# Out-projection, second normalisation, routing and sending of sequences 0 to 2 inside the attention of a transformer-like kernel on one core

## What is computed

```python
def attention(x):                      # x: (4, 1024, 128), H = 16, HD = 8
    q, k, v = (x @ W + b for each), split in heads
    scores = q.k / sqrt(8) + slope * -|kpos - qpos|, causal
    return softmax(scores).v @ Wo + bo
def moe(inputs):                       # rows n of all four sequences in one order, C = 512
    probs = softmax(x @ Wr + br); gate = max(probs); idx = argmax(probs)
    pos = cumsum(one_hot(idx)) * one_hot(idx); keep = pos < C
    h = relu((gate * x in slot pos of expert idx) @ W1 + b1); eo = h @ W2 + b2
    return gate * eo[idx, pos]
x = x + attention(layernorm(x));  x = x + moe(layernorm(x))
x = x + L1_attn(layernorm(x));    x = x + L1_ffn(layernorm(x))
```

## Time and profile before

| | |
|---|---|
| median of three runs | 726.85 us |
| profiled execution | 730.23 us, of which the span of instructions is 728.5 us |
| mean granted TensorE clock over the span | 0.867 |
| TensorE, VectorE, ScalarE, GpSimd busy over the span | 528.9, 494.2, 440.7, 243.0 us |
| last weighted sums copied | 494.9 us |
| chain that ended last, by engine | PE 43%, DVE 21%, POOL 13%, ACT 9% |

### The profile page before, as it was taken

One profiled execution on the slowest core, in us unless ns is written; L12 is line 12 of the kernel. 1 busy time (PEld: TensorE's weight loads), 2 busy tenths in 40 slices (PEclk: granted clock), 3 DMA queues, 4 the chain that ended last, 5 costly groups with the idle time before them and its releaser, 6 DMA issues.

```text
span 728.5 us, 13724 instructions
## 1 busy us (share of the span) xinstructions
PE 528.9 (73%) x4883; PEld 245.3 (34%) x4883; DVE 494.2 (68%) x964; ACT 440.7 (60%) x800; POOL 243.0 (33%) x403
## 2 busy tenths in 40 slices
PE   3675888889988998998889889884776019006774
PEld 2441333333333233332323332212665017004654
DVE  4999788889888888898888889400776206116553
ACT  1970478778877887787778778760245005007872
POOL 2651121122122122112214511210215744758552
PEclk9995699999999999999999999965775559656996
DMA  7488546522323340453232030001112133112012
GB/s 170 109 167 261 112 109 160 123 60 49 83 46 76 78 109 16 101 126 75 60 79 53 10 79 11 10 4 37 58 44 74 53 122 142 32 50 78 16 45 58
DMA packets 64906, 57.30 MB, mean 79 GB/s; under 512 B 12209, under 2 KB 55590, under 8 KB 64828
## 3 DMA queue, kind: packets, MB, share of 16 engines
q1 hardware_dynamic: 56152, 50.15, 27.8%
q10 hardware_dynamic: 6128, 2.90, 1.5%
q0 software_dynamic: 2560, 3.39, 1.4%
HBM read 29.40 MB, written 29.69 MB: 81 GB/s over the span
## 4 chain that ended last, share of the span: by engine, by line
PE 43%; DVE 21%; POOL 13%; ACT 9%; issue 9%; DMA 4%; SPq 1%; DVEq 0%; POOLq 0%; ACTq 0%
PE sums L772 16%; DVE neg_max L799 11%; PE ring L751 11%; ACT probs L820 6%; PE bank L723 6%; POOL x_rows L1044 3%; POOL expert_rows L1038 2%; PE bank L717 2%; DVE probs L517 2%; POOL rs L1059 1%; ACT xn L1485 1%; DVE v_all L525 1%; PE ring L734 1%; DMA denominators<-weighted_sums 1%; POOL max_parts L870 1%
## 5 line engine op out<-in xcount | busy, mean ns | idle before, releaser
L799 DVE TENSOR_REDUCE neg_max<-bank 128x2 f32<-128x1024 f32 (+2 forms) x320 | 342.9, 1115 | 62.0 <-PE bank L723 59.9
L820 ACT ACTIVATE probs<-ring 128x512 f32<-128x512 f32 (+4 forms) x481 | 301.9, 681 | 81.1 <-PE ring L751 68.6
L751 PE MATMUL ring<-q_operand,k_operand 56*128 56x512 bf16 (+3 forms) x768 | 165.3, 335 | 18.7 <-ACT probs L820 14.7
L772 PE MATMUL sums<-probs,v_all 128*9 128x512 f32 (+3 forms) x1536 | 164.8, 502 | 2.1 <-POOL probs L853 1.5
L853 POOL TENSOR_SCALAR_AFFINE_SELECT probs<-probs 128x512 f32<-128x512 f32 x128 | 80.2, 635 | 218.4 <-ACT probs L820 217.9
L723 PE MATMUL bank<-k_operand,q_operand 54*128 54x512 bf16 (+3 forms) x768 | 144.9, 339 | 6.9 <-DVE v_all L525 5.3
L751 PEld LDWEIGHTS ring<-q_operand,k_operand 56*128 56x128 bf16 x768 | 50.2, 94 | 154.9 <-ACT probs L820 112.6
L717 PE MATMUL bank<-masks 64*128 64x128 bf16 (+2 forms) x768 | 71.7, 223 | 5.3 <-DVE neg_max L799 4.9
L723 PEld LDWEIGHTS bank<-k_operand,q_operand 54*128 54x128 bf16 x768 | 45.9, 97 | 24.6 <-DVE neg_max L799 15.2
L717 PEld LDWEIGHTS bank<-masks 64*128 64x128 bf16 x768 | 36.5, 95 | 38.2 <-DVE neg_max L799 25.8
L772 PEld LDWEIGHTS sums<-probs,v_all 128*9 128x9 f32 x1536 | 23.3, 89 | 53.6 <-issue 40.4
(11 more groups left out here) (152 smaller groups left out, 681.5 us busy)
## 6 DMA issues: line engine op xcount, KB each, us to landing
q_operand<-q_rows SPq DMA_DIRECT2D x64, 96.0 KB, 3.7
k_operand<-k_rows SPq DMA_DIRECT2D x32, 192.0 KB, 4.4
q_rows<-qk_parts SPq DMA_DIRECT2D x36, 128.0 KB, 2.4
k_rows<-qk_parts SPq DMA_DIRECT2D x36, 128.0 KB, 2.4
expert_rows<-fill SPq DMA_DIRECT2D x16, 258.0 KB, 5.7
rows<-expert_rows SPq DMA_DIRECT2D x8, 516.0 KB, 6.5
weighted_sums<-osum SPq DMA_DIRECT2D x128, 18.0 KB
sums_in<-in_L_attn_x SPq DMA_DIRECT2D x4, 512.0 KB, 7.5
```

What stands on the lines that cost most here:

```text
L751: last = nc.tensor.matmul(psS[:, bank, w * j:w * j + w], k_op[rows, buf, p, P * kb:P * kb + P], q_op[rows, buf, c, p, q0:q0 + w], start=Tr ...
L772: last = nc.tensor.matmul(psO[32 * i:32 * i + HD + 1, q0:q0 + w], v_all[:, n, kb, i, :], probs[:, u % NPROBS, i // 2, i % 2, 0:w], start=u ...
L799: nc.vector.tensor_reduce(neg_max[:, n % 2, slot, kc, :, pairs[0]:pairs[-1] + 1, t % CH], src, AX.X, ALU.max, negate=True).then_inc(a_read, 1)
L820: nc.scalar.activation(dst, src, ACT.Exp).then_inc(ring_read, 1)
```

## The change

A fifth kind, `E`, enters the order: the entries of `EARLY_AT`, for each of sequences 0 to 2, at fixed units of the attention of the following groups. A position is (group - first group) x 12 + unit, the first group being 5, 9 or 13. The entry stands after that unit's `V`.

- The spreading of the reciprocals by matmul becomes two DMAs on SyncE: 64 KB to HBM (position 5) and 512 KB back, each head's row to eight partitions (position 7).
- `divide`, the addition of the projection, powers, scales, normalised rows and rows times gate go to GpSimd, which reads no PSUM, so ScalarE copies the projection into SBUF (`st`) first. GpSimd also issues the 8 sends of a sequence, at positions 28 to 35.
- Projection, transposes, logits and counts on TensorE take one turn each of the ring of three banks (2, 2, 1 and 1 per sequence); ScalarE copies every one of them out.
- Moments, choosing and placing stay on VectorE, in between its maxima. The counts of earlier sequences are kept as running sums, so one matmul replaces one per earlier tile.
- The clears of the slots follow the stores, one per `A`; residual rows are loaded at groups 4 to 7. The bias is added per sequence at positions 5 and 6, the last sequence's with that of sequence 2. The rows after the addition go to HBM in one DMA of 512 KB per sequence (position 21).
- The later block does sequence 3 alone, in the steps of before, without the loop of ticks. The buffers of the routing lie in a region that first holds the q and k parts of sequences 0 to 2.

```diff
+EARLY = B - 1
+EARLY_AT = {
+    4: [("reciprocals", 0)], 5: [("store_reciprocals", 0), ("bias", 0)], 6: [("bias", 1)], 7: [("load_reciprocals", 0)],
+    10: [("divide", 0)], 11: [("divide", 1), ("project", 0)], 12: [("project", 1)], 14: [("moments", 0)],
+    15: [("moments", 1), ("power", 0)], 16: [("power", 1)], 17: [("scales", 0)], 18: [("normal", 0)],
+    19: [("normal", 1), ("turned", 0)], 20: [("turned", 1)], 21: [("store_x1", 0)], 22: [("logits", 0)], 23: [("choose", 0), ("exps", 0)],
+    25: [("counts", 0)], 26: [("place", 0)], 27: [("gated", 0)], 28: [("gated", 1)],
+    **{28 + i: [("gated", 1)] * (i == 0) + [("send", i)] for i in range(KB)}}
...
+            b = (n - H // GH - 1) // (H // GH)
+            for name, c in EARLY_AT.get((n - H // GH - 1) % (H // GH) * NU + u, []) if 0 <= b < EARLY else []:
+                if name in TURNED:
+                    turn += 1
+                    order.append(("E", n, name, b, c, (head, held[head], turn)))
...
+                def load_reciprocals(b):
...
+                    sp.wait_ge(rden_out, 16 * (b + 1))
+                    sp.dma_start(r["rdb"], rden_dram[b].unsqueeze(0).to_broadcast([HD, H, S])).then_inc(rdb_in, 16)
...
-                    elif kind == "A" and n >= 5 and args[0] % 8 == 4 and clears:
+                    elif kind == "A" and clears:
                         clear_slots(sp, clears.popleft())
...
+                def project_early(b, c, bank):
...
+                    pe.wait_ge(at_ready, QC * b + c + 1)
+                    for i in range(CH):
+                        last = nc.tensor.matmul(psS[:, bank, P * i:P * i + P], ot[:, b, CW * c + P * i:CW * c + P * i + P],
+                                                w["wo"][:, :], start=True, stop=True)
+                    last.then_inc(ring_fill, 1)
...
+                def divide(b, c):
+                    pool.wait_ge(o_in[b], 32)
+                    pool.wait_ge(rdb_in, 16 * (b + 1))
+                    to = slice(CW * c, CW * c + CW)
+                    nc.gpsimd.tensor_tensor(ot[:, b, to], ot[:, b, to], r["rdb"][:, to], ALU.mult).then_inc(at_ready, 1)
+
+                def add_projected(b, c, turn):
+                    pool.wait_ge(ring_read, turn)
+                    pool.wait_ge(xb_ready, QC * b + c + 1)
...
+                def normal_early(b, c):
+                    k = QC * b + c
+                    for u in range(CH * k, CH * k + CH):
+                        last = nc.gpsimd.tensor_scalar(r["xn2"][:, u, :], rows[:, u, X1:X1 + D], r["mv2"][:, u, 0:1],
+                                                       r["nt2"][:, 1, u:u + 1], ALU.subtract, ALU.mult)
+                    last.then_inc(xn2_ready, 1)
...
+                def send(u):
...
+                    pool.wait_ge(row_ready, u + 1)
+                    nc.gpsimd.indirect_dma_start(
+                        out=slots_dram, out_offset=bass.IndirectOffsetOnAxis(ap=r["slot"][:, u:u + 1], axis=0), in_=rows[:, u, :],
+                        in_offset=None, bounds_check=E * CAP - 1, oob_is_err=False).then_inc(scattered, 16)
...
-        for u in range(TILES):
+        for u in range(KB * b, TILES):
             send_rows(u)
```

More of the change, by code:

```diff
@@ L130 @@
 VGROUP = 1
+EARLY = B - 1
[6 more added lines that the diff above has]
+    **{28 + i: [("gated", 1)] * (i == 0) + [("send", i)] for i in range(KB)}}
+TURNED = {"project": (1000, 600), "turned": (700, 600), "logits": (2000, 230), "counts": (900, 230)}
+EARLY_TIME = {"reciprocals": ("dve", 960), "moments": ("dve", 1450), "choose": ("dve", 2300), "place": ("dve", 2000),
+              "exps": ("act", 260), "bias": ("pool", 1200), "divide": ("pool", 1200), "power": ("pool", 1050),
+              "scales": ("pool", 1000), "normal": ("pool", 1600), "gated": ("pool", 1600), "send": ("pool", 1280)}
 def exp_items(u):
@@ L791, in _, with maxima @@
                 nc.vector.memset(psO, 0.0).then_inc(o_clear, 1)
-                for n in range(NG):
-                    if n >= 2:
+                def maxima(n, k):
+                    slot, t, kc, w, pairs = MAXUNITS[k]
+                    if n >= 2 and k == 0:
                         dve.wait_ge(cut_ready, QC * (n - 1))
[L796 to L804, removed]
@@ L892, in _ @@
                         cut_maxima(n, *args)
+                    elif kind == "E":
+                        name, b, c, use = args
+                        if name == "bias":
+                            add_bias(b, c)
+                            if b == EARLY - 1 and c == QC - 1:
+                                for last in range(QC):
+                                    add_bias(EARLY, last)
+                        elif name == "divide":
+                            divide(b, c)
+                        elif name == "project":
+                            add_projected(b, c, use[2])
+                        elif name == "power":
+                            power_early(b, c)
+                        elif name == "scales":
+                            scales_early(b)
+                        elif name == "normal":
+                            normal_early(b, c)
+                        elif name == "gated":
+                            gated_early(b, c)
+                        elif name == "send":
+                            send(KB * b + c)
         later_stages(nc, ctx, sb, sem, w, dict(
@@ L1005, in _ @@
     def _(sp):
-        for k in range(CHUNKS):
+        for k in LATE:
             sp.wait_ge(x1_ready, k + 1)
@@ L1192, in _ @@
-        dve.wait_ge(slot_ready, len(ROUNDS))
-        dve.wait_ge(row_ready, ROUNDS[-1][0])
-        for u in range(*ROUNDS[-1]):
+        divide(K0)
+        divide(K0 + 1)
+        for k in LATE:
+            add(k)
+        for k in LATE:
+            scales(k)
+        dve.wait_ge(fold_psum, 1)
+        nc.vector.tensor_copy(aqk[:, :], psFold[:, 0:P])
+        nc.vector.tensor_tensor(wft[:, :], psFold[:, P:2 * P], dis[:, :], ALU.add).then_inc(fold_ready, 1)
+        for k in LATE:
+            take_logits(k)
```

499 lines of the change are left out of this document (315 added, 184 removed).

## The result

| | time, us | profiled execution: span, us | granted clock, mean |
|---|---|---|---|
| before | 726.45 median (725.26 to 731.77) | 728.5 | see the earlier trace rows by stage |
| changed | 744.24 median (735.63 to 744.32) | 742.4 | 0.864 |

Changed over before: 1.0193, with a 95% interval from 1.0146 to 1.0239. The change makes the kernel about 14 us slower by this ratio (17.8 us between the medians), where 22 us less had been forecast (705).

A forecast was written before the change was run, and what follows sets the result against it. It took TensorE's fixed order, nearly full, to bound the attention and GpSimd's sends the end. 730.23 - 54 (end) + 32 (attention) = 708.2, by the median 705; own range 697 to 714, overall 690 to 724.

The forecast's parts named there:

- The end: Late part behind the attention: with only sequence 3 left there, the last send lands at 540.2 not 594.60, giving back 54 us.
- the walk: Step-by-step chain of sequence 3 from last reciprocal to last send's landing: about 34 us instead of 88, 3 us either way.
- The clears: Burst of 16 slot clears in the attention delays a DMA hop of the maxima once or twice: 1 us, between 0 and 6.
- The wait for the reciprocals' load: First half of a sequence: load lands in 5.3 us, so TensorE stands 1.5 to 2 us before the projection.
- GpSimd's 25 us a sequence: GpSimd's moved elementwise work and sends in the attention, costed at nothing because idle time ahead of masks covers them.
- the rival that was given 0.11: GpSimd's queue in the attention: masks held behind waiting entries, V matmuls behind masks; 750 us at 0.5 each; chance 0.11.
- waits in TensorE's order: Attention: 18 new TensorE entries each wait about 1 us for another engine, 723 us, parity at 1.2 each; chance 0.17.
- TensorE, VectorE and ring turns: Moved work in the attention, per sequence: TensorE 2.3 us in the first half, both engines 5.5 in the second, banks 0.5.
- absorbed: Attention: the planner's order puts new work where engines idle, cost 12 us, time 685; chance 0.16.
- Clock 1.00 in the attention: TensorE's granted clock stays 1.00 through the attention, and its new work, 6.2 us a sequence, is priced at it.
- The port rival: Attention: VectorE's two-input instructions wait for GpSimd's elementwise work, 4 us a sequence, 12 in all, time 717; chance 0.10.

The follow-up runs named there:

- y0_after: The changed kernel as it is, run once more on another chip beside the kernel before: 747.21 us, ratio 1.0103 to the kernel before.
- x3_late_sends: Changed kernel with the 24 sends of sequences 0 to 2 moved from the attention to the last block: 756.51 us, ratio 1.0395 to the kernel before.
- x1_load: Changed kernel with the reciprocals' buffer filled once from a constant table, three loads and waits gone, denominators wrong: 724.66 us, ratio 0.9948 to the kernel before.
- y5_dma: Same kernel as x5_dma, run again beside y0_after: 736.51 us, ratio 0.9946 to the kernel before.
- x2_light: Changed kernel with normalised rows moved from GpSimd to ScalarE and gated rows to VectorE: 738.46 us, ratio 1.0159 to the kernel before.
- y6_all: Same kernel as x6_all, run again beside y0_after and y5_dma: 721.33 us, ratio 0.9763 to the kernel before.
- the first set: x1_load, x2_light, x3_late_sends and x4_both: edits of the changed kernel, one cause at a time or two together, 719.84 to 756.51 us.
- the third set: y0_after, y5_dma, y6_all and x9_warm: changed kernel, two reruns of variants and a clock test, 747.21, 736.51, 721.33 and 746.59 us.
- x7_double_pe: x6_all with each early projection, transpose and logits matmul issued twice: 737.18 us, 15.6 us over x6_all.
- x8_more_dve: x6_all with 48 more unused statistics instructions on VectorE in each of three sequences' moments: 727.35 us (two runs), 5.8 us over x6_all.
- x6_all: x5_dma plus x2_light's move of normalised rows to ScalarE and gated rows to VectorE: 721.6 us, ratio 0.9734 to the kernel before.
- x9_warm: Changed kernel with five unused matmuls ahead of TensorE's wait for each sequence's first divide: 746.59 us, ratio 1.0071 to the kernel before.
- x5_dma: Changed kernel with transfers reordered, reciprocals loaded one entry earlier and used later, no computation dropped: 736.8 us, ratio 0.9956 to the kernel before.
- x4_both: Changed kernel with the edits of x1_load and x2_light together, denominators wrong: 722.02 and 719.84 us, two far longer executions left out.

## Why the prediction was wrong, step by step

**The end (54 us): right.** 33.9 us against the walk's 34.0. The last eight sends and their step are those of the earlier trace rows, and the sends of the sequence ahead did not last into it. That the sum agrees to 0.1 us is partly luck: ScalarE's normalised rows begin 9.6 us after the reciprocals and not 11.9, but both chunks' rows are on the chain (3.19 us, where 1.7 was taken).

**The clears (1 us): not contradicted.** The group with the burst of clears and the four before it take together 0.96 us more, and in y0_after 0.05 us (214.74 against 214.69).

**The wait for the reciprocals' load (2 us a sequence): failed.** The prediction said "a load of that size takes 5.3 us to land", took TensorE's stand as 1.5 to 2 us, and kept 7.3 for the first half as the end of the range. Measured: 8.30, 11.70 and 6.95 us to land, and stands of 5.6, 9.0 and 2.8 us, 17.5 in all instead of 6 (9.8 in y0_after). The 5.3 us was the median over the residual's loads of the kernel before, and was taken for another load in another place; over the nine loads of the changed kernel, y0_after and x3_late_sends it is 6.5 to 11.7 us, never 5.3. The issue was late too: 4.3 us ahead of the group's second copy of sums (237.98 and 242.30), where 5.8 had been read (234.1 and 239.94). x1_load and y5_dma show what this is worth: 14.4 us of attention when the wait is gone for nothing, 10.7 us of time when order alone hides it.

**GpSimd's 25 us a sequence (nothing): the step that failed most.** The cover named was GpSimd's idle time ahead of masks, with additions of 1.18 us as the witness. It covers a piece of 1.2 us; it does not cover the eight gated rows with the first send behind them, 6.1 us from 290.43 to the mask at 296.55, since TensorE's next V matmuls wait for that mask. The size of one instruction was taken too low as well (0.44 against 0.79 and 0.60), by a quarter of the way between rows with 4 and 512 columns. x2_light gives 8.7 us of attention for it, y6_all against y5_dma 15.2 us of time. The sends, also at nothing, cost up to 7.3 us (x3_late_sends). This is the rival that was given 0.11. It was to decide from 0.25 us an entry; by the first set it is 8.7 + 7.3 = 16 us, 0.18 us for each of 90 entries, and with the 15.2 us of the third set 22.5 us, 0.25. Whether it would have turned the sign alone is not settled; with the late load it did. The rival "waits in TensorE's order" came about too: TensorE's new entries wait 17.5 us (L882), 2.9 (L889) and 1.2 (L433), which is 1.2 us for each of 18, its figure for parity, but nearly all of it in the three projections.

**TensorE, VectorE and ring turns (8.3 us a sequence without the load): too small.** The prediction let TensorE's work go first into its idle time in the second half and took 5.5 us a sequence for it and VectorE's together. x7_double_pe and x8_more_dve give the marginal prices in the attention of x6_all, 1.0 and roughly 0.75. VectorE's moved work is 17.8 us of busy time (231.52 - 213.68), some 22 with the gaps inside its chains; the reciprocals, in the 26.1 of the prediction, were in this stretch before. So the new work is about 18.6 x 1.0 + 0.75 x (18 to 22) = 32 to 35 us, an estimate, where the prediction had 3 x (2.3 + 5.5 + 0.5) = 24.9. The rival "absorbed" falls by x7_double_pe.

**Clock 1.00 in the attention: wrong.** It is 0.92 there (before 0.97), and falls to 0.50 behind the stands. TensorE's busy time grew by 34.3 us for 18.6 of work, so by this estimate about 16 us of the attention's growth is time at a lower clock. What lowers it is not shown: keeping TensorE busy in the stands gave nothing (x9_warm), taking the stands away left the busy time as it was (x1_load), and taking GpSimd's elementwise work away shortened it by 7.8 and 9.6 us (x6_all against x5_dma, y6_all against y5_dma).

**The account.** The attention's growth of 67.9 us: 22.6 for load and elementwise work (x4_both), up to 7.3 for sends, 32 to 35 for TensorE and VectorE, 1.0 for clears: 63 to 66, each part with what it brings of the lower clock. The 2 to 5 us left lie within the spread of single executions; ring turns and GpSimd's divides and additions were not measured apart. From the last copy of sums to the reciprocals it is 11.24 us against 11.28, and from the landing to the end of the span 134.5 (607.93 to 742.4) against 133.9. So 67.9 - 54.5 + 0.6 = 14.0 us, and the spans differ by 742.4 - 728.5 = 13.9.

**The port rival: hardly seen.** The two-input instructions of the routing keep their length (225 ns, as before), because GpSimd mostly stands still beside them. The rule does show in two other kinds of instruction. Timelines of GpSimd and VectorE in the changed kernel:

```profile
282.73 0.64 POOL L1034 TENSOR_SCALAR_AFFINE_SELECT probs<-probs 128x512 f32<-128x512 f32 x1 [5.11 <-ACT probs L982]
...
282.86 0.55 DVE L1198 CAST early<-early 128x64 bf16<-128x64 f32 x1
```

```profile
531.71 0.19 DVE L1198 CAST early<-early 128x64 bf16<-128x64 f32 x1
```

Beside a mask the cast takes 0.55 us and ends with it (283.41 and 283.37); with GpSimd idle it takes 0.19. The same happens at 410.92 with 0.56, and once to a tensor_scalar of 128x4. By the rule of the Trainium skill (SBUF — State Buffer, Who interferes with whom) a VectorE instruction in a two-port mode waits until GpSimd's, if that began first, has ended, and a cast can be in such a mode; the trace agrees. It is three instructions, 1.1 us in the whole run.

## What to carry to other kernels

Work that is moved into a stretch whose order is fixed by one engine can cost that engine's time nearly one for one, however much idle time its row shows (0.92 to 1.0 here); measure the price of a microsecond there (issue something twice) before counting on the gaps. An engine's idle time ahead of a short, urgent instruction hides pieces and not a sum: here pieces of 1.2 and 3.1 us ahead of masks held up hardly any V matmul (0.3 us in all), and one of 4.7 us with a send behind it held it up for 3.2. So a queue is judged by its longest piece. A load that something waits for needs a margin for its spread (6.5 to 11.7 us here for the same 512 KB), and a place in its queue ahead of entries that themselves wait.

## What the runs showed that was not expected

- A GpSimd tensor_scalar of 128x128 f32 takes 0.79 us with two column operands and 0.60 with one; a tensor_tensor of four times the elements takes 1.18 to 1.26.
- 13.7 us of matmuls placed at TensorE's waits, which sum to 9.8 us, cost nothing that can be told (x9_warm), while 17 us placed in its order cost 15.6 (x7_double_pe).
- The same kernel's same window took 26.65 us in one execution and 29.43 in another, with the granted clock 1.00 and 0.88.
- The kernel before takes 728 us on one chip and 740 on another. The stretch behind the attention shows where, with the same code in it: it takes 179.85 us in x2_light on the first chip (554.15 to 734.0) and 185.57 in y0_after on the second (559.33 to 744.9).
